# Turning the front's input and the decoder's query shares on VectorE instead of TensorE

## What is computed

```python
xn = _layernorm(x, axis=-1)
# attention, 32 heads of 16
qkv = relu(einsum('bnc,oc->bno', xn, qkv_weight))
vk = einsum('bnhe,bnhd->bhed', v_pad, k)                 # v_pad: v and a column of ones
vk_q = einsum('bhed,bnhd->bnhe', vk, q)
y = einsum('bnc,oc->bno', vk_q[..., :D] / (vk_q[..., D:] + EPS), proj_weight) + proj_bias
# experts
spikes = sigmoid(xn @ enc_w + enc_b)                      # 512 -> 1024
cont = spikes @ s2c_w + s2c_b                             # 1024 -> 64
comb = two best of softmax(relu(cont @ r_w1 + r_b1) @ r_w2 + r_b2), rescaled
moe_out = sum over e of comb[e] * (relu(cont @ e_w1[e] + e_b1[e]) @ e_w2[e] + e_b2[e])
dec = sigmoid(sigmoid(moe_out @ c2s_w + c2s_b) @ dec_w + dec_b)   # 64 -> 1024 -> 512
x + y + (dec - mean) * rsqrt(var + 1e-5) * ln_g + ln_b
```

## Time and profile before

| | |
|---|---|
| median of three runs | 1861.84 us (1861.66 to 1862.93) |
| the profiled execution | 1862.4 us, of which the profile's span is 1860.7 us |
| PE busy | 1827.6 us, 98% of the span |
| DVE busy | 1249.8 us, 67% |
| ACT busy | 813.6 us, 44% |
| one block of the front, blocks in the middle | 28.90 us |
| one block of the decoder | 49.55 us |
| DMA, mean share of 16 engines | 0.38 to 0.49 in the front, 0.26 in the decoder |

### The profile page before, as it was taken

One profiled execution on the slowest core, in us unless ns is written; L12 is line 12 of the kernel. 1 busy time (PEld: TensorE's weight loads), 2 busy tenths in 40 slices (PEclk: granted clock), 3 DMA queues, 4 the chain that ended last, 5 costly groups with the idle time before them and its releaser, 6 DMA issues. The chain is left out here.

```text
span 1860.7 us, 25358 instructions
## 1 busy us (share of the span) xinstructions
PE 1827.6 (98%) x8756; PEld 1513.3 (81%) x8756; DVE 1249.8 (67%) x2389; ACT 813.6 (44%) x1421; POOL 408.3 (22%) x467
## 2 busy tenths in 40 slices
PE   7999999999999999999999999999999999999998
PEld 5888888888788888887787788888888888888886
DVE  6555565564578888884898655666666666666666
ACT  4555555554223444433787433333333333333333
POOL 2000000000004555520000233322222222233331
PEclk9999999999999999999999999999999999999999
DMA  5653425443224444432789531222222222222211
GB/s 221 237 204 127 198 77 224 185 164 133 75 101 173 152 153 153 153 123 84 225 249 283 155 114 52 70 78 96 96 96 97 96 97 95 79 80 90 92 52 68
DMA packets 105678, 246.42 MB, mean 132 GB/s; under 512 B 29696, under 2 KB 53328, under 8 KB 97872
## 3 DMA queue, kind: packets, MB, share of 16 engines
q1 hardware_dynamic: 97280, 236.23, 35.7%
q0 software_dynamic: 8272, 8.57, 1.7%
HBM read 161.13 MB, written 83.63 MB: 132 GB/s over the span
## 5 line engine op out<-in xcount | busy, mean ns | idle before, releaser
L672 DVE TENSOR_TENSOR spl<-sp_t,sph 128x512 fp32r<-128x512 f32 x128 | 88.6, 692 | 195.2 <-ACT sph L472 195.2
L125 PE MATMUL AB_E<-xs,enc_h 128*128 128x512 f32 x512 | 207.4, 405 | 1.2 <-DVE xs L660 1.1
L1983 PE MATMUL D_D<-dec_h,rateh 128*128 128x512 f32 x512 | 200.5, 392 | 2.2 <-DVE ratel L2091 2.2
L127 PE MATMUL AB_E<-xs,enc_h 128*128 128x512 f32 x512 | 200.3, 391 | 0.0
L126 PE MATMUL AB_E<-xs,enc_l 128*128 128x512 f32 x512 | 199.9, 390 | 0.0
L1984 PE MATMUL D_D<-dec_l,rateh 128*128 128x512 f32 x512 | 199.8, 390 | 0.0
L1985 PE MATMUL D_D<-dec_h,ratel 128*128 128x512 f32 x512 | 199.4, 389 | 0.0
L468 ACT ACTIVATE sp_t<-AB_E,cols 128x512 f32<-128x512 f32 x128 | 88.2, 689 | 201.6 <-PE AB_E L127 198.8
L1125 POOL DMA_INDIRECT slots_scratch<-ctok,idx x128 | 131.3, 1026 | 194.8 <-DVE part L1443 168.9
L1826 POOL DMA_INDIRECT ga<-eo_scratch,idx x64 | 66.4, 1038 | 482.3 <-DVE ratel L2091 466.0
L1882 ACT ACTIVATE rate<-D_Y,cols 128x512 f32<-128x512 f32 x128 | 88.1, 688 | 117.9 <-PE D_Y L1964 117.9
(11 more groups left out here) (433 smaller groups left out, 4737.4 us busy)
## 6 DMA issues: line engine op xcount, KB each, us to landing
xs_scratch<-xs SPq DMA_DIRECT2D x16, 2048.0 KB, 8.8
xsd<-xs_scratch SPq DMA_DIRECT2D x15, 2048.0 KB, 7.8
xs<-xs_scratch SPq DMA_DIRECT2D x14, 2048.0 KB, 8.2
wt<-ew_scratch SPq DMA_DIRECT2D x39, 513.0 KB, 3.9
xd<-in_x SPq DMA_DIRECT2D x16, 1024.0 KB, 5.4
out_y<-out SPq DMA_DIRECT2D x64, 256.0 KB, 2.0
x<-in_x SPq DMA_DIRECT2D x15, 1024.0 KB, 5.7
xf_scratch<-xt SPq DMA_DIRECT2D x12, 1024.0 KB, 8.4
```

The source lines that it names most:

```text
L125: pe.matmul(out, w_hi, x_hi, start=start, stop=False)
L127: return pe.matmul(out, w_hi, x_lo, start=False, stop=stop)
L672: dve.tensor_tensor(T["spl"][:, n % 3, :], T["sp_t"][:, m % 2, :], f32(T["sph"][:, n % 3, :]), ALU.subtract)\
L1983: pe.matmul(bD[t][:, :], rateh[:, n % 3, o], T["dec_h"][:, k, :], start=(k == 0), stop=False)
```

## The change

PE no longer turns blocks 2 to 15 in the front (`BY_PE = 2`: blocks 0 and 1 stay), nor the query shares of blocks 1 to 15 in the decoder (block 0 stays). Instead:
- SP issues `swap_squares`: 16 DMAs inside SBUF that put each 32x32 square at the place where its turned form belongs. In the front they move a whole block, `x` to the new buffer `xb`, 64 KB a DMA, 512 rows of 128 bytes. In the decoder they move one tile, `q` to `qb` (two slots), 16 KB a DMA, 128 rows of 128 bytes; 64 DMAs a block.
- DVE then turns every square with one `transpose` of 128x512 per chunk or tile, into the PSUM bank that PE wrote before (`turn_squares`). ACT and DVE go on from the bank as before.
- The order on ACT and DVE in the front is written anew: chunks are turned in steps 1, 2, 4, 5 and split in steps 2, 3, 5, 6, statistics stand in steps 0 to 2, the norm in steps 4 and 5. In the decoder `turned` moves one step later, and `qn` is gone: `share` writes back into `q`, so `query` of a tile waits for the swap two tiles earlier.
- `load_x` waits for the swap of the block two back, instead of its turn. `xb` has one buffer: a swap waits until the block before has been turned.
- Two waits of the first tiles' norm on POOL share one semaphore, and `s2c_raw` shares its place with `es1`.

```diff
+SQ = P // 32
+BY_PE = 2
...
         @block.sync
             def load_x(i):
-                if i >= 2:
+                if i >= 2 + BY_PE:
+                    sp.wait_ge(S["xb_in"], 16 * SQ * SQ * (i - 1 - BY_PE))
+                elif i >= 2:
                     sp.wait_ge(S["turned"], (i - 2) * KC + KC)
...
+            def swap_squares(i):
+                sp.wait_ge(S["norm_out"], i * NT + NT)
+                if i > BY_PE:
+                    sp.wait_ge(S["turned"], i * KC)
+                for tq in range(SQ):
+                    tokens = x[i % 2][tq * 32:(tq + 1) * 32, :, :].rearrange("p t (c f n) -> p (t c) f n", c=KC, f=SQ)
+                    for fq in range(SQ):
+                        sp.dma_start(T["xb"][fq * 32:(fq + 1) * 32, :, tq * 32:(tq + 1) * 32], tokens[:, :, fq, :])\
+                            .then_inc(S["xb_in"], 16)
...
             for i in range(NB):
                 if i + 2 < NB:
                     load_x(i + 2)
+                if BY_PE <= i + 1 < NB:
+                    swap_squares(i + 1)
...
         @block.vector
+            def turn_squares(i, c):
+                n = i * KC + c
+                if c == 0:
+                    dve.wait_ge(S["xb_in"], 16 * SQ * SQ * (i + 1 - BY_PE))
+                dve.wait_ge(S["xl_out"], n - 1)
+                wait(dve, S["xt_out"], sum(k // KC in IN_PAIRS for k in range(n - 1)))
+                dve.transpose(bT[c % 2][:, :].rearrange("p (t n) -> p t n", t=NT),
+                              T["xb"][:, :, :].rearrange("p (t c) n -> p c t n", c=KC)[:, c, :, :]).then_inc(S["turned"], 1)
...
+                    if i and i + 1 < NB:
+                        if m in (1, 2, 4, 5):
+                            turn_squares(i + 1, m - 1 - m // 4)
+                    if i and i + 2 < NB:
+                        for t in ((0, 1), (2,), (3,), (), (), (), (), ())[m]:
+                            stats(i + 2, t)
+                        for t in ((), (), (), (), (0, 1, 2), (3,), (), ())[m]:
+                            norm(i + 2, t)
+                    if i and i + 1 < NB:
+                        if m in (2, 3, 5, 6):
+                            turn(i + 1, m - 2 - m // 5)
...
 decode, @block.sync
+            def swap_squares(i, t):
+                n = i * NT + t
+                sp.wait_ge(S["qn_out"], n + 1)
+                sp.wait_ge(S["turn_done"], n - 1)
+                for tq in range(SQ):
+                    tokens = q[tq * 32:(tq + 1) * 32, n % 2, :].rearrange("p (c f n) -> p c f n", c=KC, f=SQ)
+                    for fq in range(SQ):
+                        sp.dma_start(qb[fq * 32:(fq + 1) * 32, n % 2, :, tq * 32:(tq + 1) * 32], tokens[:, :, fq, :])\
+                            .then_inc(S[f"part_in{t}"], 16)
...
             for i in range(NB + 1):
+                if i + 1 < NB:
+                    for t in range(NT):
+                        swap_squares(i + 1, t)
                 if i + 2 < NB:
                     load_xs(i + 2)
...
 decode, @block.scalar
             def query(i, t):
                 act.wait_ge(S["q_done"], n + 1)
-                wait(act, S["qn_out"], n - 1)
+                if n >= NT + 2:
+                    act.wait_ge(*swapped(n - 2))
...
 decode, @block.vector
+            def turn_squares(i, t):
+                n = i * NT + t
+                dve.wait_ge(*swapped(n))
+                dve.wait_ge(S["qnl_out"], n)
+                dve.transpose(bR[:, :], qb[:, n % 2, :, :].rearrange("p g n -> p (g n)")).then_inc(S["turn_done"], 1)
...
-                        if 2 <= s <= NT + 1:
-                            turned(i + 1, s - 2)
+                        late = 3 if has_dec else 2
+                        if late <= s < NT + late:
+                            turned(i + 1, s - late)
...
+                    if has_att and has_dec and 2 <= s <= NT + 1:
+                        turn_squares(i + 1, s - 2)
```

More of the change, by code:

```diff
@@ L185, in place @@
         put("A", f"x{i}", [P, NT, DIM])
+    put("A", "xb", [P, NT * KC, P])
     for i in range(2):
@@ L205, in place @@
         put("A", f"e2_raw{i}", [P, EC, MOE])
-        put("A", f"es{i}", [P, 2 * EH + 2], F32R)
+        at = put("A", f"es{i}", [P, 2 * EH + 2], F32R)
+    m["s2c_raw"] = nc.alloc_sbuf_tensor_at("s2c_raw", [P, HC, P], F32, offset=at)
     split("beC", "wp", [P, KC, DIM])
@@ L419, in _ @@
                 pool.tensor_tensor(T["ve"][:, o], T["mv"][:, t, 1:2], T["eps"][:, o], ALU.add)\
-                    .then_inc(S["ve_out" if last else "ve_first"], 1)
-                pool.wait_ge(S["ve_out" if last else "ve_first"], 1 if last else t + 1)
+                    .then_inc(S["ve_out" if last else "rs_first"], 1)
+                pool.wait_ge(S["ve_out" if last else "rs_first"], 1 if last else 2 * t + 1)
                 pool.tensor_tensor(T["rs"][:, o], T["ve"][:, o], T["half_down"][:, o], ALU.pow)\
@@ L500, in _ @@
                     encode(i, m)
[L501 to L507, removed]
+                    if i == 0 and m > 4:
+                        keep(1, m - 5)
+                    if i == 1 and m == 0:
+                        keep(1, KC - 1)
+                    if i and i + 1 < NB and m in (4, 7):
+                        keep(i + 1, 1 if m == 4 else 3)
                     if m == 1 and i:
@@ L517, in _ @@
                             turn(1, m - 4)
-                        elif i and m % 2:
-                            turn(i + 1, m // 2)
+                        elif i and m in (2, 3, 5, 6):
+                            turn(i + 1, m - 2 - m // 5)
+                            if m in (3, 6):
+                                keep(i + 1, m // 3 * 2 - 2)
                     if 1 <= i <= 8 and m == 6:
@@ L616, in _ @@
                         logits(i - 1)
[L617 to L621, removed]
+                    if i == 0 and m >= 4:
+                        turn(1, m - 4)
             content(NB - 1, HC - 2)
@@ L762, in _ @@
                         logits(i - 1)
[L763 to L778, removed]
+                    if i == 0 and m >= 4:
+                        turn(1, m - 4)
+                    if i == 0 and 2 <= m <= 4:
+                        for t in ((0,), (1,), (2, 3))[m - 2]:
+                            stats(2, t)
+                    if i == 0 and m >= 5:
+                        for t in ((0,), (1, 2), (3,))[m - 5]:
+                            norm(2, t)
+                    if i and i + 1 < NB:
[8 more added lines that the diff above has]
+                        if m in (2, 3, 5, 6):
+                            turn(i + 1, m - 2 - m // 5)
                     if 1 <= i <= 8 and m == 7:
@@ L781, in _ @@
                         weights(n, c, KC + 1 + i)
-                    if i >= 8 and m == 5:
+                    if i >= 8 and m == 7:
                         e = i - 8
@@ L1760, in decode @@
         xs, rate, rateh, ratel = (T[n] for n in ("xsd", "rate", "rateh", "ratel"))
-        q, qk, qn, qnh, qnl = (T[n] for n in ("q", "qk", "qn", "qnh", "qnl"))
+        q, qk, qb, qnh, qnl = (T[n] for n in ("q", "qk", "qb", "qnh", "qnl"))
         x, out = [T[f"xd{i}"] for i in range(3)], [T[f"out{i}"] for i in range(2)]
@@ L1764, in decode, with swapped @@
         heads = [P, HEADS, HD]
+        def swapped(n):
+            i, t = divmod(n, NT)
+            loads = 16 + 32 * len(range(t, NS, NT))
+            return S[f"part_in{t}"], loads + 16 * SQ * SQ * i
         def stages(i):
@@ L1862, in query @@
                 act.wait_ge(S["q_done"], n + 1)
-                wait(act, S["qn_out"], n - 1)
+                if n >= NT + 2:
+                    act.wait_ge(*swapped(n - 2))
+                else:
+                    wait(act, S["turn_done"], n - 1)
                 act.activation(q[:, n % 2, :], bX[t % 2][:, :], ACT.Relu).then_inc(S["q_out"], 1)
@@ L1932, in turn @@
                 for g in range(KC):
-                    k = pe.transpose(bR[:, g * P:(g + 1) * P], qn[:, n % 2, g * P:(g + 1) * P], T["ident"][:, :])
+                    k = pe.transpose(bR[:, g * P:(g + 1) * P], q[:, n % 2, g * P:(g + 1) * P], T["ident"][:, :])
                 k.then_inc(S["turn_done"], 1)
@@ L2009, in _ @@
                             attend(i + 1, s - NT)
-                        if 1 <= s <= NT:
-                            turn(i + 1, s - 1)
+                        if not has_dec and 1 <= s <= NT:
+                            turn(0, s - 1)
             last = NB - 1
```

8 lines of the change are left out of this document (3 added, 5 removed).

## The result

The changed kernel takes **2085.59 us** (median of four runs, 2082.65 to 2087.06), the kernel before, in runs beside it, 1861.75 us (1861.09 to 1862.93). The ratio is 1.120, 95% interval 1.118 to 1.122: 12% slower, where the prediction said 1825 us and at most 1912. The profiled execution took 2082.65 us, its span is 2080.9 us.

The account below looks back on a forecast made before the run. PE was taken to bound both stages. From 1862.4 us, -22 in the front (-28 + 3 + 3) and -15.5 in the decoder (-28.5 + 13) gave 1824.9, stated as 1825 us; range 1806 to 1912.

Parts of the forecast that it names:

- What leaves PE: Front and decoder: 56 turns of 0.5 us and 60 of 0.475 us leave PE, 56.5 us if replacements are hidden.
- down by some 55 us at any outcome: Sign to look for over the whole kernel: PE's busy time falls by some 55 us, whichever outcome comes.
- The transpose on DVE: Both stages: one 128x512 transpose per turn takes 0.61 us, 2.4 us a block, which DVE's spare time hides.
- The rival of a slow transpose: Both stages: a transpose takes twice 0.61 us, costing 17 us in the front and 2 in the decoder: 1844; chance 0.05.
- The front's swap: Front: sixteen DMAs a block take 14.0 us, steady blocks lose nothing; the front gains 22 us in all.
- d: Spacing of swap DMA starts on SP: 0.80 us in the front (0.56 to 1.12), 0.42 in the decoder (0.37 to 0.46).
- the ring: Front: cycle of swap, then DVE's work from first transpose to the norm starting another swap; 25.8 us against PE's 26.9.
- 3 us for the first swap: Front, block 2: some 11 us until PE needs `spl`, 14.0 to wait for, so 3 us lost once.
- 3 us for SP's fuller queue: Front, from block 9: SP also issues eight expert transfers a block; it fits, but costs 3 us over five blocks.
- The decoder's swaps: Decoder: 64 DMAs a block, hidden up to 26.0 us; the excess costs 13 us over 15 blocks, leaving -15.5 us.
- PE waits for `midl` at the end of a block: Decoder sign: late swaps delay `midl`, which PE needs at the start of step 7, 35.9 us after step 1 starts.
- SP becomes the bound of the decoder: Decoder rival: swaps start 0.46 us apart, costing 51 us against 28.5 gained; 1863 with the front's -22; chance 0.13.

Follow-up runs that it names:

- e4_issue_cost: No kernel computation: SP issues six DMAs of each of several shapes, in a row or awaited singly; no shape in a row under 0.59 us in the median.
- e5_via_dram: Changed kernel, each decoder query tile moved through DRAM by one store and four loads instead of sixteen swaps: 1815.24 us, ratio 0.975.

## Why the prediction was wrong

- **What leaves PE: right.** 27.05 us a front block and 47.6 us a decoder block (with half the squares, or by way of DRAM) against the 26.9 and 47.65 forecast. PE's busy time fell by 51 us (1776.2 in the kernel by way of DRAM), but only there. In the changed kernel it rose by 51, mostly because a matmul at half clock counts for longer (0.63 us against 0.39 in the lines above); the sign "down by some 55 us at any outcome" was wrong.
- **The transpose on DVE: near.** 0.72 us busy and 0.63 from its start to that of the next, for 0.61 taken. The rival of a slow transpose has fallen.

By the 311 ns for a 128x128 bf16 square of the Trainium skill ("VectorE: DVE Perf Modes", The three transpose paths) the estimate was 1.24 us for an instruction. The lines of the trace have 0.72 us in float32 and into PSUM; so an instruction of four squares in float32 does not cost four times the Trainium skill's figure for one in bf16.

- **The front's swap: right in mechanism, and nearly in size.** d was 0.67, inside 0.56 to 1.12 and under the 0.87 from which the ring bounds; cutting the DMAs in two made it bound where and as the formula says. The sum was -22 and -18.0 came. The term "3 us for the first swap" had the wrong place: the loss was at the third swap, behind the store of zeros, 6.6 us. The 3 us for SP's fuller queue from block 9 on did not come: 27.05 us from swap to swap there too (317.76 to 344.81). What is left is the block, 1.85 us shorter instead of 2, which is 25.9 us in 14 blocks.
- **The decoder's swaps: the step that failed.** The forecast for the decoder was -15.5 us and +241.8 came. The condition (64 d up to 26.0 us) and the slope (64 us of block per us of d) held in size, the first in part by luck, since PE was held by `rate` before the middle and not by `midl` before step 7. The sign "PE waits for `midl` at the end of a block" was wrong with it. The value of d was not right: "I take 0.42", with a high end of 0.46, against 0.658 measured. The working of it: 64 x (0.658 - 0.42) = 15.2 us a block, 228 us in 15 blocks. This term alone takes 1825 to 2053. The low end came from an isolated store of a whole tile to DRAM, the high end from whole loads out of DRAM. I let the small size of the moves (128 rows) count for them. For the front I had taken the strided issue of 518 ns as low end in the same prediction; in the decoder the same row would have given 64 x 0.56 - 26.0 = 9.8 us a block, 147 us, and a clear "slower". The range of d was not made of the nearest rows, but of those with the same number of rows.
- **The clock: not in the sum.** Once SP made PE wait, the granted clock fell to half for 3.4 or 6.8 us at a time, and where that lay on the path it cost time, 2.3 us in the block shown. The mean block was 65.6 us, (1964.7 - 1046.4) / 14 from the loads of `xsd`, and 47.65 - 26.0 + 42.1 = 63.8: 1.8 us a block, 27 us; that all of it is the clock's is worked out from the stretches above, and no run was made without the clock's fall. With 2053 and the 4 us that the front fell short, this is 2084 of the 2085.6.
- **A reading.** Relu to `ratel` is 3.80 us by the rows (1339.54 - 1335.74), not 3.85; it is in no term of the sum.
- **The rivals.** "SP becomes the bound of the decoder" was the right one, with the right place, at 1863 instead of 2086. Its price ended at the high end of d.

The Trainium skill's rule ("DMA: Bandwidth & Descriptors", Rules for kernel authors) that small transfers should become one large one spoke against this change, and the runs agree: 16 KB and 4 KB a DMA cost the same 0.6 us of queue, and five DMAs instead of sixteen turned +242 us into -28.6 (1843.8 to 1815.2).

The chance of 0.31 for slower, and a range of 1806 to 1912, were both too sure of one number that no row showed.

## What to carry to other kernels

Count a queue's DMAs, not their bytes, and price each by the dearest issue that the trace has for a move of any likeness; then multiply before you choose, since with 64 in a row a tenth of a microsecond is 6.4 us a block. Write down from which price the queue becomes the bound (here 0.41 us); when a row of the same trace, 0.52, is already above it, that is the forecast. When a queue gets new work that others wait for, look for the one large transfer that already stands in it.

## What the runs showed of the hardware

- In a row, a DMA inside SBUF held SP for 0.59 to 0.64 us in the median, from one 32x32 square to a whole 128x512 tile (`e4_issue_cost`); awaited one by one the whole tile took 465 ns, the decoder's square move 586.
- A DVE transpose of 32x32 squares over 128x512 in float32 took 720 ns from SBUF into PSUM, 727 in the decoder, like a plain pass of the same size.
- With 5 MB of stores in its queue, the next issue held SP for 16.98 us, at a DMA share near 1 (`e5_via_dram`).
- Around waits of PE of some microseconds its granted clock was 0.5 for 3.4 or 6.8 us at a time, beginning within the wait in the one shown; in the changed kernel such pieces add up to 227 us of the span, and PE's busy time rose with 464 instructions less.
